# A graph network's flow stage, with the due ticks of its four chains written anew

## The reference, cut to what matters

```python
h = jnp.maximum(_layernorm(x, axis=-1), 0.0)
x = x + _L0_gnn_ref(h, adj, adj, ...)   # filters made of each pair's distance, summed over neighbours
h = jnp.maximum(_layernorm(x, axis=-1), 0.0)
x = x + _L1_gnn_ref(h, adj, ...)        # hyperbolic: Moebius matvec, log map of each pair, attention, exp map
h = jnp.maximum(_layernorm(x, axis=-1), 0.0)
x = x + _L2_gnn_ref(h, adj, ...)        # degree-normalised adjacency, times x, times W
h = jnp.maximum(_layernorm(x, axis=-1), 0.0)
x = x + _L3_gnn_ref(h, adj, ...)        # mean of the messages over the senders, then an update
```

## Time and profile before

| | us |
|---|---|
| median of two executions | 2825.57 |
| the profiled execution | 2826.92 |
| its span | 2824.9 |
| its flow stage ahead of PE's first attention | about 1454 to 1554.47 |
| slots 0 to 7, to the tanh of the weights (L1170) behind each | 142.3, 141.7, 152.0, 148.8, 146.7, 146.4, 142.0, 130 |
| behind the last dots | 2704.4 to 2824.9 |

### The profile page before, as it was taken

How to read it: one execution, slowest core, us unless ns; L and a number is a source line. 1 busy time by engine, 2 the same in 40 slices (tenths; PEclk the granted TensorE clock), 3 DMA queues, 4 the chain that set the end, 5 groups by cost and what they waited for, 6 DMA issues and landing times. The chain is left out here.

```text
span 2824.9 us, 53482 instructions
## 1 busy us (share of the span) xinstructions
PE 2575.6 (91%) x21008; PEld 1077.0 (38%) x21008; DVE 2198.6 (78%) x3639; ACT 2162.7 (77%) x2136; POOL 1704.4 (60%) x773
## 2 busy tenths in 40 slices
PE   4899999999999999999962999999999999999963
PEld 2333333333333333333332334344443435343433
DVE  6698998989989899898978365768687878774356
ACT  6888888888888888888842676877787878777643
POOL 0798898988988899898953334343434343433211
PEclk9999999999999999999985999999999999999976
DMA  9899999989999899898813455445455545454410
GB/s 235 183 224 245 237 255 247 205 196 202 196 196 202 194 199 202 195 198 197 180 38 70 96 126 131 106 115 115 116 123 127 117 118 126 116 120 109 94 45 19
DMA packets 247241, 438.99 MB, mean 155 GB/s; under 512 B 86752, under 2 KB 212320, under 8 KB 213344
## 3 DMA queue, kind: packets, MB, share of 16 engines
q1 hardware_dynamic: 246992, 435.57, 67.4%
HBM read 402.98 MB, written 48.23 MB: 160 GB/s over the span
## 5 line engine op out<-in xcount | busy, mean ns | idle before, releaser
L691 POOL TENSOR_TENSOR f_gate<-rfT,f_sq 128x1024 f32<-128x1024 f32 x512 | 1218.3, 2380 | 226.6 <-DVE f_prod L706 151.6
L624 PE MATMUL PS<-f_h,w_W2T 64*64 64x512 f32 x8192 | 998.4, 591 | 9.7 <-PE PS L624 1.9
L706 DVE SCALAR_TENSOR_TENSOR f_prod<-PS,b2l,f_gate 128x1024 f32<-128x1024 f32 x512 | 657.3, 1284 | 146.3 <-PE PS L624 110.4
L1164 ACT ACTIVATE a_silu<-PS,c_att_b 128x1024 f32<-128x1024 f32 x512 | 543.1, 1110 | 247.3 <-PE PS L1012 246.5
L586 ACT ACTIVATE f_h<-PS,c_b 128x1024 f32<-128x1024 f32 x512 | 556.6, 1113 | 166.6 <-PE PS L606 165.9
L698 DVE TENSOR_REDUCE yT<-f_prod 128x16 f32<-128x1024 f32 x512 | 618.7, 1209 | 0.0
L1324 POOL TENSOR_TENSOR a_vd<-n_vt,jmask 128x1024 f32<-128x1024 f32 x128 | 255.9, 2000 | 543.2 <-PE PS L1012 543.2
L624 PEld LDWEIGHTS PS<-f_h,w_W2T 64*64 64x64 f32 x8192 | 340.5, 133 | 561.4 <-issue 435.9
L606 PE MATMUL PS<-f_gauss,W1two 64*64 64x512 f32 x4096 | 545.8, 594 | 7.4 <-ACT f_gauss L573 4.8
L1008 PE MATMUL PS<-a_vd,a_hw 32*128 32x512 f32 x2048 | 397.6, 656 | 52.0 <-ACT a_silu L1164 24.8
L1012 PE MATMUL PS<-a_ud,a_own 32*128 32x512 f32 x2048 | 367.9, 603 | 0.0
(11 more groups left out here) (251 smaller groups left out, 2261.8 us busy)
## 6 DMA issues: line engine op xcount, KB each, us to landing
f_gauss<-in_adj SPq DMA_DIRECT2D x128, 1024.0 KB, 11.7
f_sq<-adj_sq SPq DMA_DIRECT2D x256, 512.0 KB, 10.0
a_ud<-ud_d SPq DMA_DIRECT2D x128, 512.0 KB, 6.3
a_own<-own_d SPq DMA_DIRECT2D x256, 64.0 KB, 1.9
b_x<-in_x SPq DMA_DIRECT2D x8, 512.0 KB, 4.6
x_d<-b_x SPq DMA_DIRECT2D x8, 512.0 KB, 3.9
h_d<-b_h SPq DMA_DIRECT2D x8, 512.0 KB, 7.3
hw_d<-b_xc SPq DMA_DIRECT2D x8, 512.0 KB, 6.9
```

The source lines that it names most:

```text
L624: PE.matmul(post("message", c)[rows[b], n, :], W2T[rows[k], rows[fh]], hidden(c, n)[rows[k], b, :], start=not second, stop=bool(second)).t ...
L691: GP.tensor_tensor(by_pair(GATE[c % GATE_BUFS][:]), rf, by_pair(squares), ALU.mult).then_inc(s_gate, 1)
L706: V.scalar_tensor_tensor(PR[c % PR_BUFS][:], post("message", c).rearrange("p b n -> p (b n)"), b2l[:, c % 2:c % 2 + 1], GATE[c % GATE_BUFS ...
L1164: A.activation(SI[p % SI_BUFS][:], PS[:, first:first + 2, :].rearrange("p b n -> p (b n)"), ACT.Silu, bias=cols["att_b1"][:]).then_inc(s_s ...
```

## The change

All due ticks of the four chains are written anew, on all five engines: the table `FILLS` for PE, and the numbers behind `yield` in the programs of SP, ACT, POOL and DVE. Within a chain the operations keep their order. No operation, buffer, semaphore or wait is added or taken away. `AHEAD`, the attention's ticks and the weights' tanh at tick 2 stay. In FILLS the chains move later:

```diff
 FILLS = {
-    "lead": (("y0", 32.0625), ("y1", 35), ("t0", 41), ("t1", 43), ("m0", 45), ("m1", 46)),
-    "pair": (("h0", 9), ("h1", 11), ("g", 13), ("y", 21), ("r0", 23), ("r1", 25), ("r2", 29), ("r3", 31)),
-    "mix": (("u0", 18), ("u1", 18.0625), ("v0", 31.0625), ("v1", 31.125), ("s0", 32), ("s1", 35.0625),
-             ("a0", 35.125), ("a1", 36), ("z0", 38.0625), ("z1", 38.125)),
-    "last": (("l0", 15), ("l1", 17), ("k0", 19), ("k1", 27), ("t0", 37), ("t1", 38), ("p0", 40), ("p1", 42),
-             ("p2", 42.0625), ("p3", 47), ("q0", 49), ("q1", 51), ("e0", 51.0625), ("e1", 55)),
+    "lead": (("y0", 42), ("y1", 46), ("t0", 50), ("t1", 50.0625), ("m0", 51.125), ("m1", 59)),
+    "pair": (("h0", 27), ("h1", 29), ("g", 30), ("y", 30.0625), ("r0", 34.125), ("r1", 34.1875),
+             ("r2", 36.0625), ("r3", 37)),
+    "mix": (("u0", 29.0625), ("u1", 34), ("v0", 38), ("v1", 38.0625), ("s0", 40), ("s1", 44),
+             ("a0", 44.0625), ("a1", 45), ("z0", 45.0625), ("z1", 48)),
+    "last": (("l0", 32), ("l1", 34.0625), ("k0", 36), ("k1", 36.125), ("t0", 47), ("t1", 48.0625),
+             ("p0", 49), ("p1", 51), ("p2", 51.0625), ("p3", 55), ("q0", 55.0625), ("q1", 60),
+             ("e0", 60.0625), ("e1", 61)),
 }
```

More of the change, by code:

```diff
@@ L1208, in pair @@
             for h in range(2):
-                yield (9, 11)[h]
+                yield (27, 29.0625)[h]
                 evacuate(num[f"h{h}"], half(bHT, h))
-            yield 11.0625
+            yield 29.125
             for h in range(2):
@@ L1214, in pair @@
             A.activation(bMX[:], bHT[:], ACT.Square).then_inc(b["hsq"], 1)
-            yield 13
+            yield 33.0625
             evacuate(num["g"], ba[:], scale=-2.0, bias=1.0)
-            yield 21
+            yield 33.125
             filled(A, num["y"])
@@ L1388, in last @@
         def last(g):
-            yield 20
+            yield 36
             GP.wait_ge(f["relu"], 4 * g + 4)
@@ L1499, in lead @@
             recip(sB("zr"), sB("zr"))
-            yield 53.4375
+            yield 64.3125
             series(sB("o"), sB("q"))
-            yield 54.375
+            yield 65.75
             tt(sB("e1"), sB("n2"), sB("n2"), MU)
             tt(sB("d4"), sB("d4"), sB("rstd"), MU)
-            yield 55.0625
+            yield 67
             V.wait_ge(b["ln"], g + 1)
             stt(sB("w"), sB("w"), 0.5, sB("zr"), MU, MU)
-            yield 56.3125
+            yield 67.5
             blend(sB("o"), sB("w"), sB("q"), sB("msk"))
-            yield 57.3125
+            yield 68.4375
             tt(sB("o"), sB("o"), sB("z"), MU)
@@ L1575, in pair @@
             recip(e3, e3)
-            yield 12.25
+            yield 26.1875
             tt(e2, e2, e3, MU)
@@ L1579, in pair @@
             tt(e3, e3, x2, MU)
-            yield 12.5
+            yield 27.8125
             series(e1, e3)
-            yield 13.125
+            yield 29.625
             tt(e1, e1, e2, MU)
             tt(cs_all[:, g, :], e1, x2_1, MU, gives=(b["lin"], g))
-            yield 20.875
+            yield 30.375
             taken(V, num["g"])
@@ L1600, in pair @@
             ts(bden[:], bden[:], MIN_NORM, MA)
-            yield 30.75
+            yield 37.0625
             recip(bden[:], bden[:], gives=(b["den"], g))
-            yield 32.5625
+            yield 40.5625
             stt(bq[:], bq[:], 0.0, bden[:], MA, MU, gives=(b["q"], g))
-            yield 33
+            yield 41
             ts(bT[:], bq[:], 1.0 / 11, MU)
-            for k, at in ((9, 33.4375), (7, 34.0625), (5, 35.3125), (3, 35.625)):
+            for k, at in ((9, 41.1875), (7, 41.5625), (5, 41.9375), (3, 42.5)):
                 yield at
                 stt(bT[:], bT[:], 1.0 / k, bq[:], AD, MU)
-            yield 36.5
+            yield 42.875
             ts(bT[:], bT[:], 1.0, AD)
-            yield 37.1875
+            yield 43.8125
             V.wait_ge(b["z"], g + 1)
@@ L1668, in mix @@
             recip(sF("lam"), sF("lam"))
-            yield 42.1875
+            yield 49.3125
             V.wait_ge(f["hu"], g + 1)
             rsum(sF("hu"), fXC[:])
-            yield 42.9375
+            yield 51.125
             V.wait_ge(f["sqrt1"], g + 1)
@@ L1687, in mix @@
             ts(sF("den"), sF("den"), MIN_NORM, MA)
-            yield 45.875
+            yield 55.1875
             recip(sF("den"), sF("den"))
-            yield 46.5625
+            yield 55.8125
             tt(sF("cu"), sF("x2_1"), sF("f"), MU)
@@ L1723, in mix @@
             recip(sF("zi"), sF("zi"))
-            yield 54.5
+            yield 65.0625
             series(sF("o"), sF("q"))
-            yield 55.8125
+            yield 66.9375
             V.wait_ge(f["ln"], g + 1)
             stt(sF("w"), sF("w"), 0.5, sF("zr"), MU, MU)
-            yield 56.9375
+            yield 67.0625
             blend(sF("o"), sF("w"), sF("q"), sF("msk"))
-            yield 57.5625
+            yield 67.9375
             tt(sF("o"), sF("o"), sF("z"), MU)
@@ L1735, in mix @@
             tt(sF("ch"), sF("ch"), sF("o"), MU)
-            yield 58.5625
+            yield 68.75
             tt(sF("cu"), sF("cu"), sF("o"), MU, gives=(f["cu"], g))
-            yield 59.6875
+            yield 69.75
             tt(fH[:], fH[:], of_nodes(sF("ch")), MU)
-            yield 61.0625
+            yield 71.375
             V.wait_ge(f["uc"], g + 1)
             tt(fH[:], fH[:], fUU[:], AD, gives=(f["h"], g))
-            yield 63.5625
+            yield 74.9375
             V.wait_ge(f["xsq"], g + 1)
             rsum(sF("n3"), fSQ[:], gives=(f["n3"], g))
-            yield 65.625
+            yield 76.25
             V.wait_ge(f["sqrt3"], g + 1)
@@ L1810, in last @@
                 for h in range(2):
-                    yield {36: (55.1875, 57.9375), 39: (61.875, 64.4375)}[first][h]
+                    yield {36: (59.75, 65.9375), 39: (68.8125, 72.375)}[first][h]
                     n = num[f"{name}{h}"]
```

210 lines of the change are left out of this document (105 added, 105 removed).

## The result

The changed kernel takes 2932.14 us (median of two, 2931.28 to 2932.99) where the kernel before takes 2825.57: ratio 1.0377, 95% interval 1.0333 to 1.0422. That is 107 us more. The forecast was 2849 with a range of 2806 to 2884: the sign was right, the size was not, and the range didn't hold the time.

A forecast was written before the change was run, and what follows sets the result against it. Inside the slots PE's pace was taken to bound the kernel, with two silus setting a bare step. Terms 23 + 31 - 7 - 22 - 5 + 3 = +23 gave 2849 us, range 2806 to 2884.

The forecast's parts named there:

- (5): Ahead of slot 0, first attention 3 us sooner and a Sqrt trip gone: -5; later U and row loads covered by 8 us.
- (6): Behind the last silu: mix(6)'s chain and load of fH later, +9.4, mix(7) returns about 6.5; net +3.
- (3): Table trips and small waits in bare steps: some go, new ones at ticks 63 and 77 and q0 come; -7.
- (1): Fills packed into fewer steps of every slot, so bare steps no longer hide 0.64 us of a fill each: +23.
- Rival D: Packing costs nothing, ACT's work is covered, and the four early waits go: 2795 us, chance 0.08.
- (2): ACT's work crowded in ticks 45 to 51 exceeds PE's work there, 4.7 us a full slot: +31.
- rival B: New waits at tick 49 bring the clock down, about 3.3 us more in seven slots: 2872 us, chance 0.14.
- (4): The four long PE waits for a silu in slots 0 to 3, 13.2 us idle, go: -22.
- test for the clock: Granted clock under 0.95 in slots 2 to 5 would show the forecast wrong, in favour of rival B.

The follow-up runs named there:

- x1_load24: Changed kernel with mix's loads of adj, adjT and fH written on SP at tick 24, ahead of the row loads of tick 25: 2893.02 us.
- x3_both: Changed kernel with mix's loads at tick 24 on SP and fill q0 at tick 58 instead of 55.0625 on PE: 2884.45 us.
- w1_ln65: x3_both with the lead's Ln on ACT at tick 65 instead of 63, next to mix's Ln: 2885.11 us.
- y6_packed: Kernel before with four fills (h0, g, y, k1) packed into steps that have a fill already: 2838.97 us, ratio 1.0048.
- x4_before14: Kernel before with mix's loads and the attention's store and load moved on SP to four ticks ahead of u0: 2823.07 us, ratio 0.9997.
- z3_before_apart: Kernel before with mix's second Sqrt on ACT at tick 50.0625 instead of 49.0625: 2844.14 us, ratio 1.0073.
- y2_relus: x3_both with DVE's bias3 at tick 38.5 and half of the eight relus at tick 43 on ACT: 2884.36 us.
- z4_t1: x3_both with last's fill t1 on PE at tick 47.0625 instead of 48.0625: 2881.53 us.
- y1_joined: x3_both with the pair's two Ln on ACT at tick 45.1875 instead of 47.0625, right behind its Sqrt: 2892.49 us.
- v3_joined_e0: Kernel before with the lead's Ln at tick 53 instead of 51, next to mix's Ln, and fill e0 at 53: 2817.16 us, ratio 0.9982.

## Why the prediction was wrong

**Missing from the parts: what the moved transfers wait for (48 us).** Under (5) the prediction followed the stores and the row loads; for the load of fH it looked only at the tail (6). It had not set the place of this load, behind the row loads of tick 25, against u0 at tick 29 on PE and mix's start at 23.19 on DVE. The row loads wait for the attention, and the load lands 8 us after its issue. That is the step that failed: a wait put at nothing without a reason, and x1_load24 prices it at 39 us. In (3), q0 at 55.06 ahead of DVE's p2 at 57.125 was seen, and priced at +1 a slot; it cost 4.3 net in slot 4 and 9 to 11 over all: PE waits 2.58 us there, and the clock falls behind it (0.63 from 2313.15 to 2317.80). Without these two the time is 2884.45, at the upper end of the range.

**(1), packing, +23: right as far as it was tried.** Bare steps from tick 7 to 27 take 3.38 and 3.74 as before, but for one behind the Sqrts of tick 13, and the run with four fills packed gave 13.6 where the same price makes 17. Rival D is out. One count is off by one: from dots to dots the fills of before touch 22 steps, not 23, so six are lost and the term is nearer to +20.

**(2), crowding, +31: the mechanism is right, its form is not.** The waits at ticks 47 to 53 came (1.08, 1.06, 1.10, 0.64 us in slot 4, 3.9 together for the 4.7 forecast). Left out was the clock, named as rival B with 3.3 us; where it fell it cost 2.7. The forecast put it aside because a wait of 1 us had not brought it down as those of the earlier trace rows did; two of 1.06 and 1.10 behind each other did in some slots and not in others: in slot 3 of the changed kernel (11.02 us) but not in its slots 2, 4 and 5 (8.34 and 8.35), in slots 2, 4 and 5 of x1_load24 but not in its slot 3, in slots 2 to 5 of x3_both. The single cause named, one load more between Sqrt and Ln, was wrong as a remedy: joined, they cost the same.

**(3), trips in bare steps, -7: not shown.** The step behind the Ln of 63 and 65 takes 7.57 us (6.08 before), as such pricing has it. In w1_ln65 the excess goes and the total stays, because the clock then falls in the step behind it. In the changed kernel it falls there with the excess in place (4.33 to 5.59 us in slots 2 to 6), so what the excess costs there wasn't measured. An excess read from one step counts only if its neighbours are read too. E0's wait of 0.78 for DVE wasn't in the sum.

**(4), the four early waits, -22: too large.** Slots 2 and 3 of the kernel before hold 5.3 and 2.1 us over slot 4. Both waits are also gone in y6_packed (slot 2: 148.6 us) and in x4_before14 (147.1 and 148.2), and the total of x4_before14 is that of the kernel before. So they hang on small shifts. Slot 1 kept a like wait in another form (1.85 us in x3_both), slot 0 one of 1.91. Some 7 of 22 were there to be had, by one execution; z3_before_apart shows that moving a trip off such a wait may cost more than the wait.

**(5) and (6)** hold within 3 us: the first attention starts at 1552.72 (forecast about 1551, before 1554.47), no slot but the first starts with a wait for a_ud or a_hw, and the tail is 1.2 us longer for the forecast +3. SP's load of fH comes 17.6 us behind the end of the last dots, as forecast (17), though the chain in (6) adds up to 2723.8 and not 2721.9. How the rest of the tail gives it back was not followed: PE waits 24.66 us for f_uu in one piece.

Put together: only the 48 us of the load and q0 are measured. Some 35 are left between 2849 and x3_both. Some 15 in term (4), by slot lengths, and some 15 for the clock in the crowded steps of x3_both, by one step of slot 4, would fill them, but that sum isn't shown: (2) with its clock would then be 31 + 15, and taking the trips out gave 18 net. How the 61 us between the kernel before and x3_both divide stays open.

The prediction's test for the clock, "under 0.95 in slots 2 to 5", would have missed it: slots 2 to 5 stand at 0.97, 0.95, 0.97 and 0.97. The fall is in single steps, 0.85 and 0.82 in slot 4 and 0.72 in that of x3_both.

## What to carry to other kernels

When an order is written anew, list for each transfer what stands in front of it in its queue and what that waits for, then its landing, and compare that with every reader. A distance in due ticks alone didn't tell (x4_before14); a place behind or ahead of one waiting instruction was worth 39 us. Where PE is busy for 90% of a slot and ACT and DVE for 70 to 80%, moving work from one gap to another mostly exchanged waits (six runs against x3_both, 3 us at best). The one version that was faster shares a table load and puts a fill into a bare step. And read a step in every slot before it explains a total: the same waits cost 8.35 us in one slot and 11.02 in the next.

## What the runs showed of the hardware

- TensorE's clock fell from the higher of its levels to the lower after idle times of 2.58 and 3.58 us (slot 4 of the changed kernel), and also around two of 1.06 and 1.10 us with 1.13 us of work between: in x1_load24 the matmul group behind the second took 1.22 us, and 0.70 in slot 4 of the changed kernel, where the same two waits left the clock up.
- The same idle time at the same place of one kernel ended either way. In the kernel before PE waits 2.64 us for the weights' tanh at the start of slots 2 to 6. At the start of slot 3 the clock stayed up (1.00 over the step of 2.92 us), at that of slot 4 it fell (0.65 over 4.37 us):

```profile
1991.27 1.07 PE L1027 MATMUL PS<-a_silu,w2sel 128*32 128x512 f32 x8 [2.64 <-ACT a_att L1170]
...
2140.04 1.94 PE L1027 MATMUL PS<-a_silu,w2sel 128*32 128x512 f32 x8 [2.64 <-ACT a_att L1170]
```

  Why stays open. In several runs a fall that was gone from one step stood in another (y2_relus, z4_t1, w1_ln65), so a step of one execution says little about a change of 1 or 2 us a slot.
- A load of 512 KB on SP's queue, issued behind seven row loads, ended its reader's wait 8.2 us after the start of its issue (2224.30 to 2232.50), 4.02 of it in the issue itself; in x1_load24, ahead of the row loads, the issue took 0.37 and the landing came after 4.5 us. In the kernel before its issue took 1.27, but the load of adjT just ahead of it took 4.32 (at 2153.89).
- The Sqrt and the Ln each had a table load of 1.28 us with no silu between them (2249.91 and 2252.62 in y1_joined), while two Ln (v3_joined_e0), or two Sqrt (2200.77 in the changed kernel), shared one.
